# Expert stages of an eight-layer hybrid stack: 128-row tiles held in the array, weights streamed past them from a copy kept in SBUF

## The chip, the cores and the metric

One Trainium2 chip, of which one core runs the program. Matrices go through TensorE (PE, with PEld its weight loads), element work through VectorE (DVE), ScalarE (ACT) and GpSimd (POOL); SyncE (SP) starts the direct transfers. The metric is device microseconds of the whole program, the median of several runs; smaller is better.

## The reference

2048 tokens of 128 numbers pass eight layers, called a to h here: a state-space layer, experts (b), local attention with a feed-forward part, experts (d), sliding attention, full attention with experts (f), a hologram layer, full attention with experts (h). Layers b and d call the first function below with 9 experts and an inner width of 352; layers f and h end with the lines of the second one, with 8 experts, an inner width of 256, and one shared expert that every token passes.

```python
def _L0_ffn_ref(x, Wr, Wg, Wu, Wd):
    probs = jax.nn.softmax(jnp.einsum('bsh,he->bse', x, Wr), axis=-1)
    topk_w, topk_idx = jax.lax.top_k(probs, TOP_K)            # TOP_K = 2
    topk_w = topk_w / jnp.sum(topk_w, axis=-1, keepdims=True)
    cw = jnp.zeros((T, E), dtype=x.dtype).at[jnp.arange(T)[:, None], idxf].add(wf)
    gate = jax.nn.silu(jnp.einsum('th,ehi->tei', xf, Wg))
    hidden = gate * jnp.einsum('th,ehi->tei', xf, Wu)
    return jnp.einsum('tei,eih,te->th', hidden, Wd, cw).reshape(B, S, H)

# _L1_ffn_ref, after its attention
shared = swiglu(h2, sh_gate, sh_up, sh_down)
eout = jnp.einsum('etf,efd->etd', jax.nn.silu(gate) * up, e_down)
moe_out = (shared + jnp.einsum('etd,te->td', eout, combine)).reshape(B, S, d)
```

## The kernel before

Each layer is a chain of stages. A stage is one block in which every engine has its own program in a fixed, written order; engines meet through semaphores, and a stage begins when all engines have left the one before. An expert layer has these two stages:

- **norm_stage** with a router. DVE normalises 16 tiles of 128 tokens in four groups (L352 to L370), POOL takes the inverse roots (L391, L393), PE transposes the tiles (L428) and multiplies them by the router (L418), ACT copies the transposed banks (L445, L447), DVE ranks the experts (`rank`, L337 to L343). SP stores the normalised rows to `h_rows` in HBM (L1752); the stage waits for these stores. In layers f and h, ACT and POOL also split the shared expert's weights here (L452, L398), and POOL then adds the attention's result to `x` (L400).
- **experts_stage**. `dispatch` on DVE (L1919 to L1979) sorts the 4096 pairs of token and chosen expert into blocks of 256 rows of one expert, each padded at its end: 24 blocks for 9 experts, 23 for 8. It ends with two lists of row numbers per block. Then a loop over the blocks follows, in `block_steps`' order. In f and h, eight shared blocks of 256 consecutive tokens are woven in.

For one routed block b of the loop:

- POOL starts two indirect transfers that gather 128 rows each from `h_rows` (L2131), three blocks ahead (`AHEAD`), and at its end two that scatter the results to `e_rows` (L2138). POOL does `gather(b + 3)` and then `scatter(b)`.
- SP reads the block's expert into a register and loads its three matrices (L1733 to L1737) into one of three buffers (`RAW`), once block b - 3 has left the array.
- PE transposes the rows (`turn`, L1839). ACT and DVE split the turned rows into a high and a low part in the fp32r format (L1891 or L1893, L2007 or L2009), and they split the block's weights in the same way (`high_weights` L1883, `low_weights` L2000). Three passes over these parts, high by high, high by low and low by high, give a product close to fp32.
- PE computes J chunks of up to 128 inner columns (`up`, L1861): a piece of the weights is held in the array and the 256 turned rows stream past, for gate and up, three passes each, so 6 matmuls a chunk. ACT takes the silu (L1902), DVE multiplies it with up (L2018). The result lies with the inner columns on the partitions, which is what `down` (L1871) needs as its held operand.
- DVE copies the output to `rows_out` (L2032) or, for a shared block, adds it to `x` (L2028).

After the loop SP loads the scattered rows back in token order (L2062), and DVE adds them to `x` with the routing weights (L2041).

Of the kernel before, what the change touches and what calls it, by code (L numbers as in the profile page):

```python
# [60 lines left out]
BLOCK = 256  # L61
SHARED_BLOCKS = N_TOK // BLOCK
RAW = 3
GATHERS = 4
AHEAD = 3
SCATTERS = 3
# [236 lines left out]
def norm_stage(c, src, dst, rms=False, transpose=False, scale=None, shift=None, first=False, router=None, onto=None,  # L303
               shared=None):
# [20 lines left out]
    with nc.Block() as block:  # L325
# [61 lines left out]
        def _(pool):  # L387
            for g in range(CHUNKS):
# [5 lines left out]
                    .then_inc(rstd_ready.sem, 1)  # L394
            if shared is not None:
# [6 lines left out]
        if router is not None:  # L402
            @block.sync
            def _(sp):
                if shared is not None:
                    load_weights(sp, c.shared_raw, c.shared_down, shared, shared_loaded)
                store_rows(c, sp, dst)
# [14 lines left out]
        if transpose:  # L422
# [14 lines left out]
            def _(act):  # L437
                for b in range(CHUNKS):
# [10 lines left out]
                    if shared is not None and b == 0:  # L449
                        act.wait_ge(*shared_loaded.after(loads_of_expert(shared[0].shape[1]) * 16))  # L450
# [11 lines left out]
    if shared is not None:  # L462
        high_ready.passed(CHUNKS)
        shared_loaded.passed(16 * loads_of_expert(shared[0].shape[1]))
# [1244 lines left out]
def routed_blocks(E):  # L1709

    return (2 * N_TOK + E * (BLOCK - 1)) // BLOCK


def block_steps(blocks, shared):
# [3 lines left out]
    steps = [("shared", 0), ("shared", 1)]  # L1718
    done = 2
    for b in range(blocks):  # L1720
        steps.append(("routed", b))
        if b % 3 == 2 and done < SHARED_BLOCKS - 1:
            steps.append(("shared", done))
            done += 1
    return steps + [("shared", s) for s in range(done, SHARED_BLOCKS)]


def load_weights(sp, raw, down, weights, loaded):

    g, u, d = weights  # L1730
    inner = g.shape[1]
    whole = inner // P
    sp.dma_start(raw[:, 0, :], g).then_inc(loaded.sem, 16)  # L1733
    sp.dma_start(raw[:, 1, :], u).then_inc(loaded.sem, 16)
    sp.dma_start(down[:, 0:whole, :], d[0:whole * P, :].rearrange("(j p) d -> p j d", p=P)).then_inc(loaded.sem, 16)
    if inner % P:
        sp.dma_start(down[0:inner % P, whole, :], d[whole * P:inner, :]).then_inc(loaded.sem, 16)  # L1737


def loads_of_expert(inner):  # L1740

    return 3 + (1 if inner % P else 0)
# [13 lines left out]
def experts_stage(c, E, soft_of_probs, gate_w, up_w, down_w, inner, scale=None, shared=False):  # L1756
# [12 lines left out]
    COLUMNS = 2 * BLOCKS  # L1769
    LOADS = loads_of_expert(inner)  # L1770
# [4 lines left out]
    UNITS = len(steps) * J  # L1775
# [9 lines left out]
    weights_loaded = [c.count(f"moe_weights_loaded_{b}") for b in range(RAW)]  # L1785
    weights_high = c.count("moe_weights_high_ready")
# [6 lines left out]
    up_ready = c.count("moe_up_ready")  # L1793
    silu_ready = c.count("moe_silu_ready")
    hid_ready = c.count("moe_hidden_ready")
# [4 lines left out]
    links = [0]  # L1800
# [617 lines left out]
```

## Time and profile before

| | before |
|---|---|
| median of 3 runs | 2829.86 us (2827.12 to 2830.12) |
| the profiled execution | 2829.18 us, span 2827.5 us |
| PE busy | 2208.4 us (78%) |
| DVE busy | 2130.7 us (75%) |
| ACT busy | 1471.3 us (52%) |
| POOL busy | 611.3 us (22%) |
| mean granted TensorE clock | 0.865 |

The shares are means over the whole program. Nearly half of the span is the head loops of the two full attentions, in which DVE is busy all the time; the expert stages are four short stretches, and what limits them is read in those stretches alone. Spans of PE are modelled as pipelined, so a busy PE is not at its peak. A clock of 1.00 stands for 2.4 GHz, 0.50 for 1.2 GHz.

### The profile page before, as it was taken

The page shows a single profiled execution, that of the slowest core. Times are in us where ns is not written, and L with a number is a line of the kernel's source. Part 1 is how long each engine was busy: PE and PEld are TensorE (multiplying, and loading weights), DVE is VectorE, ACT ScalarE, POOL GpSimd, SP SyncE. Part 2 cuts the span into 40 slices and gives each one's busy share as a digit, 9 for nine tenths or more (in the row PEclk, how much of TensorE's full clock was granted, in tenths as well). Part 3 has the DMA queues.
Part 4 walks back from the last instruction along what each step waited for, and adds up shares of the span by engine and source line. Part 5 has one row for each costly group of instructions (what it writes and reads, how often), then busy time and mean ns, then how long its engine had stood idle before and what let it go on. Part 6 is the DMA issues. An engine that isn't in the chain of part 4 may idle for free. (4 is left out here: it accounts for less than half of the span.)

```text
span 2827.5 us, 44830 instructions
## 1 busy us (share of the span) xinstructions
PE 2208.4 (78%) x16030; PEld 983.4 (35%) x16030; DVE 2130.7 (75%) x5328; ACT 1471.3 (52%) x2014; POOL 611.3 (22%) x877
## 2 busy tenths in 40 slices
PE   6477368757558599999999976737999999999574
PEld 2376235556425312122212225622121222221474
DVE  7733687453468599999999936458999999996654
ACT  2133236323125327777777773311777777778332
POOL 5256221235411100000000014730000000000274
PEclk8578679868769769999999997865899999999698
DMA  2144272033364131101110002414010111010144
GB/s 59 46 115 123 56 128 38 13 92 116 101 102 82 19 106 24 24 13 24 24 24 12 13 18 83 120 48 123 13 24 16 21 24 24 15 22 2 44 120 118
DMA packets 133454, 154.46 MB, mean 55 GB/s; under 512 B 25674, under 2 KB 110672, under 8 KB 133232
## 3 DMA queue, kind: packets, MB, share of 16 engines
q1 hardware_dynamic: 119664, 126.30, 19.4%
q0 software_dynamic: 13568, 25.30, 3.1%
q8 instruction: 127, 2.08, 0.3%
q14 instruction: 95, 0.78, 0.1%
HBM read 106.72 MB, written 42.80 MB: 53 GB/s over the span
## 5 line engine op out<-in xcount | busy, mean ns | idle before, releaser
L1167 DVE TENSOR_REDUCE pair_mx<-ps 128x1 f32<-128x512 f32 x2048 | 1270.8, 683 | 21.6 <-PE ps L1010 17.3
L1139 ACT ACTIVATE prob<-ps 128x1024 f32<-128x1024 f32 x1024 | 990.0, 1021 | 249.7 <-PE ps L1045 248.0
L1010 PE MATMUL ps<-k_stack,q_stack 48*128 48x512 bf16 x2048 | 643.0, 404 | 56.1 <-PEq L828 13.7
L1059 PE MATMUL ps<-prob,v_head 128*32 128x512 f32 x4096 | 547.5, 607 | 1.3 <-ACT prob L1139 1.0
L1010 PEld LDWEIGHTS ps<-k_stack,q_stack 48*128 48x128 bf16 x2048 | 148.6, 93 | 903.1 <-DVE pair_mx L1167 842.1
L1045 PE MATMUL ps<-q_stack,k_stack 51*128 51x512 bf16 x2048 | 438.4, 383 | 8.7 <-ACT prob L1139 5.3
L1861 PE MATMUL ps<-block_part,weight_part 128*128 128x256 f32 (+1 forms) x1416 | 250.5, 328 | 44.8 <-DVE weight_part L2000 42.6
L1861 PEld LDWEIGHTS ps<-block_part,weight_part 128*128 128x128 f32 (+1 forms) x1416 | 215.3, 219 | 52.7 <-DVE weight_part L2000 48.8
L2138 POOL DMA_INDIRECT e_rows<-rows_out,scatter_ids x188 | 189.1, 1006 | 167.4 <-DVE rows_out L2032 129.7
L2131 POOL DMA_INDIRECT rows_in<-h_rows,gather_ids x188 | 190.0, 1011 | 156.2 <-DVE scatter_ids L1979 100.2
L2018 DVE TENSOR_TENSOR hid<-silu,ps 128x256 f32<-128x256 f32 (+1 forms) x268 | 109.7, 417 | 149.4 <-ACT silu L1902 148.7
L1190 POOL CAST shift<-rowmax 128x16 bf16<-128x16 f32 x32 | 6.3, 197 | 991.2 <-DVE rowmax L1171 991.2
L1514 DVE CUSTOM_DVE_ANT_0 ps<-ps,mask 128x256 f32<-128x256 f32 (+2 forms) x512 | 179.8, 419 | 45.1 <-PE ps L1320 42.8
L1902 ACT ACTIVATE silu<-ps 128x256 f32<-128x256 f32 (+1 forms) x268 | 98.9, 380 | 169.4 <-PE ps L1861 166.5
L2000 DVE TENSOR_TENSOR weight_part<-weight_raw,weight_part 128x352 fp32r<-128x352 f32 (+1 forms) x188 | 88.8, 473 | 128.8 <-ACT weight_part L1883 128.8
L1883 ACT ACTIVATE weight_part<-weight_raw 128x352 fp32r<-128x352 f32 (+1 forms) x188 | 85.1, 454 | 180.0 <-DMA down_raw<-in_L_ffn_Wd_dram 150.0
L1478 ACT ACTIVATE prob<-ps 128x1024 f32<-128x1024 f32 (+1 forms) x128 | 114.4, 917 | 78.2 <-PE ps L1368 78.1
L1871 PE MATMUL ps<-down_raw,hid 128*128 128x128 f32 x944 | 152.3, 320 | 3.5 <-DVE hid L2018 2.7
L1871 PEld LDWEIGHTS ps<-down_raw,hid 128*128 128x128 f32 x944 | 143.0, 234 | 8.0 <-DVE hid L2018 7.6
L1839 PE MATMUL ps<-ident,rows_in 128*128 128x128 f32 x188 | 45.7, 331 | 114.9 <-DMA rows_in<-h_rows,gather_ids 114.7
L1045 PEld LDWEIGHTS ps<-q_stack,k_stack 51*128 51x128 bf16 x2048 | 105.2, 94 | 62.7 <-ACT prob L1139 45.9
L1059 PEld LDWEIGHTS ps<-prob,v_head 128*32 128x32 f32 x4096 | 80.7, 108 | 120.5 <-issue 117.3
(233 smaller groups left out, 2038.2 us busy)
## 6 DMA issues: line engine op xcount, KB each, us to landing
k_stack<-image_dram SPq DMA_DIRECT2D x96, 192.0 KB, 4.2
q_stack<-image_dram SPq DMA_DIRECT2D x88, 192.0 KB, 4.5
weight_raw<-in_L_ffn_Wg_dram SPq DMA_DIRECT2D x48, 176.0 KB
weight_raw<-in_L_ffn_Wu_dram SPq DMA_DIRECT2D x48, 176.0 KB
results<-e_rows SPq DMA_DIRECT2D x32, 256.0 KB, 4.7
down_raw<-in_L_ffn_Wd_dram SPq DMA_DIRECT2D x48, 128.0 KB
weight_raw<-in_L_ffn_e_gate_dram SPq DMA_DIRECT2D x46, 128.0 KB
weight_raw<-in_L_ffn_e_up_dram SPq DMA_DIRECT2D x46, 128.0 KB
```

Source lines behind the costliest of these rows:

```text
L1010: nc.tensor.matmul(max_bank(n), rows_of(c.q_stack, b, g, ROWS, slice(t * P, (t + 1) * P)), rows_of(c.k_stack, b, g, ROWS, slice(k * CHUNK, ...
L1045: ins = nc.tensor.matmul(bank(c, 2 * (u % 2) + g), rows_of(c.k_stack, b, g, EXP_ROWS, slice(kb * P, (kb + 1) * P)), rows_of(c.q_stack, b, ...
L1059: ins = nc.tensor.matmul(out, c.v_head[:, e % 2, kb, :], unit, start=(kb == 0), stop=(kb == TILES - 1), skip_group_check=True)
L1139: nc.scalar.activation(c.prob[:, u % P_UNITS, :], c.ps[:, 2 * (u % 2) * CHUNK:2 * (u % 2) * CHUNK + UNIT], ACT.Exp, scale=scale).then_inc( ...
L1167: nc.vector.reduce_max(mx[:, w:w + 1], max_bank(n), AX.X).then_inc(max_taken.sem, 1)
L1478: nc.scalar.activation(probs, scores, ACT.Exp, scale=scale).then_inc(exp_done.sem, 1)
L1514: ins = nc.vector.tensor_tensor_reduce(scores, scores, c.mask32[:, window, P - back:WIDE], 1.0, LOWEST, ALU.add, ALU.max, accum_out=mx[:, ...
L1861: ins = nc.tensor.matmul(out[0:m, k * BLOCK:(k + 1) * BLOCK], w, x, start=(a == 0), stop=(a == 2))
L1871: ins = nc.tensor.matmul(bank(c, 4 + n % 2)[:, t * P:(t + 1) * P], c.hid[0:sizes[j], n % 2, j, t * P:(t + 1) * P], down_weights(n, j), sta ...
L2018: nc.vector.tensor_tensor(c.hid[0:m, n % 2, j, :], c.silu[0:m, unit % 2, :], bank(c, unit % 4)[0:m, BLOCK:2 * BLOCK], ALU.mult).then_inc(h ...
L2131: pool.indirect_dma_start(c.rows_in[:, b % GATHERS, t, :], None, c.h_rows[:, :], bass.IndirectOffsetOnAxis(ap=c.gather_ids[:, 2 * b + t:2 ...
L2138: pool.indirect_dma_start(c.e_rows[:, :], bass.IndirectOffsetOnAxis(ap=c.scatter_ids[:, 2 * b + t:2 * b + t + 1], axis=0), c.rows_out[:, b ...
```

## The change

Only the norm stages with a router and the expert stages change. A routed unit is now a tile of 128 rows of one expert: 40 tiles for 9 experts, 39 for 8, and 16 shared tiles instead of 8 shared blocks. The turned rows are held in the array and the weights stream past, so one matmul is 352 (or 256) columns long and `hid` comes out with the tokens on the partitions; it has to be transposed on PE, and copied by ACT, before `down` can use it. All experts' weights are loaded by SP in the norm stage, ahead of the stores of the rows; ACT rounds them to the high part there, and POOL subtracts to get the low part, for five experts in the norm stage and for the others at the start of the expert stage. In the loop no weights are loaded or split: PE reads the expert of each tile into a register and forms the address of the weights from it.

```diff
-BLOCK = 256
-SHARED_BLOCKS = N_TOK // BLOCK
-RAW = 3
-GATHERS = 4
-AHEAD = 3
-SCATTERS = 3
+GROUP = 3
+EARLY = 5
+GATHERS = 8
+AHEAD = 6
+SCATTERS = 5
...
+            if weights is not None:
+                for e in range(EARLY):
+                    low_weights(c, pool, e)
...
+                load_all_weights(c, sp, weights)
                 store_rows(c, sp, dst)
...
+                    if weights is not None and b:
+                        high_weights(c, act, b - 1, weights[0].shape[0], weights[0].shape[2])
...
+def high_weights(c, act, group, E, inner):
+
+    first, n = expert_groups(E)[group]
+    act.wait_ge(*c.count(f"moe_weights_loaded_{group}").after(n * loads_of_expert(inner) * 16 + 32))
+    for e in range(first, first + n):
+        c.nc.scalar.activation(c.weight_high[:, e], c.weight_raw[:, e], ACT.Copy).then_inc(c.count("moe_weights_high_ready").sem, 1)
...
+def low_weights(c, pool, e):
+
+    pool.wait_ge(*c.count("moe_weights_high_ready").after(e + 1))
+    pool.tensor_tensor(c.weight_raw[:, e].bitcast(fp32r), c.weight_raw[:, e], c.weight_high[:, e], ALU.subtract)\
+        .then_inc(c.count("moe_weights_split").sem, 1)
...
+        if n >= 0:
+            for j in range(J):
+                ins = nc.tensor.transpose(out[:, j * P:(j + 1) * P], c.hid[:, n % 2, j * P:(j + 1) * P], c.ident[:])
+        if b is not None:
+            ins = nc.tensor.transpose(out[:, 3 * P:4 * P], c.rows_in[:, b % GATHERS, :], c.ident[:])
...
+                    part = c.weight_high if v == 0 else c.weight_low
+                    x = c.block_part[:, b % 2, u, :]
+                    w = part[:, bass.ds(expert[b], 1), k, :].rearrange("p o i -> p (o i)")
+                ins = nc.tensor.matmul(bank(c, 2 * (n % 2) + k, inner), x, w, start=(a == 0), stop=(a == 2))
...
+            for n in range(N + 2):
+                if n < N:
+                    up(pe, n)
+                if n >= 2:
+                    down(pe, n - 2)
+                if any(turns(n - 1)):
+                    turn(pe, n - 1)
...
+                pool.indirect_dma_start(c.rows_in[:, b % GATHERS, :], None, c.h_rows[:, :],
+                                        bass.IndirectOffsetOnAxis(ap=c.gather_ids[:, b:b + 1], axis=0))\
+                    .then_inc(gathered[b % GATHERS].sem, 16)
...
+            for e in range(EARLY, E):
+                low_weights(c, pool, e)
             pool.wait_ge(*ids_ready.after(2))
```

Three places show how the order of instructions moves. On PE, one block of layer b in the steady part of the loop stood before as follows; the brackets name the semaphores that an instruction waits for.

```order
L1861 MATMUL ps<-block_part,weight_part 128x256 [waits moe_hidden_ready,moe_ht_split,moe_weights_split]
L1861 MATMUL ps<-block_part,weight_part 128x256 x5
L1839 MATMUL ps<-ident,rows_in 128x128 [waits moe_gathered_1]
L1839 MATMUL ps<-ident,rows_in 128x128
L1861 MATMUL ps<-block_part,weight_part 128x256 [waits moe_hidden_ready]
L1861 MATMUL ps<-block_part,weight_part 128x256 x5
L1871 MATMUL ps<-down_raw,hid 128x128 [waits moe_out_taken,moe_hidden_ready]
L1871 MATMUL ps<-down_raw,hid 128x128 x5
L1861 MATMUL ps<-block_part,weight_part 96x256 [waits moe_hidden_ready]
L1861 MATMUL ps<-block_part,weight_part 96x256 x5
```

With the change one tile, half of such a block, stands there like this (the register rows are ISA and REGISTER_ALU).

```order
L1901 ISA [waits moe_hidden_ready,moe_ht_split]
L1901 MATMUL ps<-weight_high,block_part 128x352
L1901 REGISTER_ALU
L1901 MATMUL ps<-weight_raw,block_part 128x352
L1901 MATMUL ps<-weight_high,block_part 128x352
L1916 ISA [waits moe_hidden_turned]
L1916 MATMUL ps<-down,hidt 128x128
L1916 ISA
L1916 MATMUL ps<-down,hidt 128x128
L1879 MATMUL ps<-ident,hid 128x128 [waits moe_gathered_5,moe_hidden_ready]
L1879 MATMUL ps<-ident,hid 128x128 x2
L1881 MATMUL ps<-ident,rows_in 128x128
```

(The five rows of L1901 come twice, for gate and up, and a third pair of L1916 follows the two shown.) The wait for the split weights is gone from the loop, three transposes of `hid` and seven register rows have come in, and the transposes of step n - 1 now wait for the rows of tile n + 2.

On POOL, the end of the norm stage and the start of the expert stage of layer b stood before as follows.

```order
L393 TENSOR_TENSOR rstd<-rstd,minus_half 128x4 [waits norm_rstd_ready]
L325 UNCONDITIONAL_BRANCH
L2125 UNCONDITIONAL_BRANCH [waits barrier_Pool_Activation_PE_DVE_SP_gather]
L2131 DMA rows_in<-h_rows,gather_ids 128x128 [waits moe_ids_ready]
L2131 DMA rows_in<-h_rows,gather_ids 128x128 x7
L2138 DMA e_rows<-rows_out,scatter_ids 10240x128 [waits moe_out_taken]
L2138 DMA e_rows<-rows_out,scatter_ids 10240x128
L2131 DMA rows_in<-h_rows,gather_ids 128x128 [waits moe_turned]
L2131 DMA rows_in<-h_rows,gather_ids 128x128
```

The same place with the change:

```order
L392 TENSOR_TENSOR rstd<-rstd,minus_half 128x4 [waits norm_rstd_ready]
L1770 TENSOR_TENSOR weight_raw<-weight_raw,weight_high 128x704 [waits moe_weights_high_ready] x5
L324 UNCONDITIONAL_BRANCH
L2149 UNCONDITIONAL_BRANCH [waits barrier_Pool_Activation_PE_DVE_SP_gather]
L1770 TENSOR_TENSOR weight_raw<-weight_raw,weight_high 128x704 [waits moe_weights_high_ready] x4
L2154 DMA rows_in<-h_rows,gather_ids 128x128 [waits moe_ids_ready]
L2154 DMA rows_in<-h_rows,gather_ids 128x128 x6
L2160 DMA e_rows<-rows_out,scatter_ids 9216x128 [waits moe_out_taken]
L2154 DMA rows_in<-h_rows,gather_ids 128x128
L2160 DMA e_rows<-rows_out,scatter_ids 9216x128 [waits moe_out_taken]
```

Nine subtractions have come in, five before the stage's end and four ahead of the first gather; in the loop one gather and one scatter alternate for 40 tiles, where there were two and two for 24 blocks.

On SP, the norm stage of layer b held only the stores of the rows between its two branches.

```order
L403 UNCONDITIONAL_BRANCH [waits barrier_Pool_Activation_PE_DVE_SP_release]
L1752 DMA h_rows<-h 128x4x128 [waits norm_tile_ready] x4
L325 UNCONDITIONAL_BRANCH [waits norm_rows_stored]
```

With the change the loads of the last of three groups of experts and the stores read:

```order
L1738 DMA weight_raw<-in_L_ffn_Wg_dram 128x3x352
L1739 DMA weight_raw<-in_L_ffn_Wu_dram 128x3x352
L1741 DMA down<-in_L_ffn_Wd_dram 128x2x128
L1743 DMA down<-in_L_ffn_Wd_dram 96x128
L1741 DMA down<-in_L_ffn_Wd_dram 128x2x128
L1743 DMA down<-in_L_ffn_Wd_dram 96x128
L1741 DMA down<-in_L_ffn_Wd_dram 128x2x128
L1743 DMA down<-in_L_ffn_Wd_dram 96x128
L1786 DMA h_rows<-h 128x4x128 [waits norm_tile_ready] x4
```

So 24 loads stand ahead of the four stores, on the same queue, and the stage still waits for the stores.

## Rows read from the trace of the kernel before

**Rows 1.** The head of the page: the span of the profiled execution.
```profile
span 2827.5 us, 44830 instructions
```

**Rows 2.** Loops b, d, f, h: PE, PEld, DVE, ACT, POOL busy, clock, DMA, GB/s.
```profile
127.78:295.98 168.20, 118.42 (x768) 112.22 (x768) 67.08 (x171) 51.79 (x143) 98.59 (x96) 0.79 0.36 105
588.50:760.56 172.06, 118.80 (x768) 112.98 (x768) 66.56 (x171) 51.79 (x143) 96.42 (x96) 0.79 0.36 103
1721.85:1854.57 132.72, 99.14 (x659) 91.50 (x657) 62.57 (x170) 49.28 (x133) 91.89 (x92) 0.86 0.36 105
2677.25:2804.03 126.78, 92.92 (x651) 85.92 (x649) 61.78 (x169) 49.30 (x133) 90.21 (x90) 0.92 0.37 109
```

**Rows 3.** Groups by line and form: busy, mean ns | idle before, released by.
```profile
L2138 POOL DMA_INDIRECT e_rows<-rows_out,scatter_ids x188 | 189.1, 1006 | 167.4 <-DVE rows_out L2032 129.7
L1883 ACT ACTIVATE weight_part<-weight_raw 128x352 fp32r<-128x352 f32 x96 | 47.3, 494 | 153.3 <-DMA down_raw<-in_L_ffn_Wd_dram 150.0 <-PE ps L1861 3.3
L2018 DVE TENSOR_TENSOR hid<-silu,ps 128x256 f32<-128x256 f32 x220 | 91.7, 417 | 86.4 <-ACT silu L1902 85.7
```

**Rows 4.** Timeline of POOL in layer b: start, us, [idle before].
```profile
127.78 1.22 POOL L2131 DMA_INDIRECT rows_in<-h_rows,gather_ids  x1 [25.30 <-DVE scatter_ids L1979]
143.36 1.00 POOL L2138 DMA_INDIRECT e_rows<-rows_out,scatter_ids  x1 [5.53 <-DVE rows_out L2032]
295.01 0.97 POOL L2138 DMA_INDIRECT e_rows<-rows_out,scatter_ids  x1 [0.30 <-issue]
```

**Rows 5.** Timeline of PE's weight loads in layer b, at both clocks.
```profile
143.26 1.42 PEld L1871 LDWEIGHTS ps<-down_raw,hid 128*128 128x128 f32 x12
144.61 0.75 PEld L1861 LDWEIGHTS ps<-block_part,weight_part 128*96 128x96 f32 x6
...
206.72 0.29 PEld L1839 LDWEIGHTS ps<-ident,rows_in 128*128 128x128 f32 x2 [3.53 <-DMA rows_in<-h_rows,gather_ids]
206.99 1.40 PEld L1861 LDWEIGHTS ps<-block_part,weight_part 128*128 128x128 f32 x6
208.28 1.88 PEld L1871 LDWEIGHTS ps<-down_raw,hid 128*128 128x128 f32 x10
```

**Rows 6.** Short stretches: columns as in rows 2; the last is the results' reload.
```profile
142.00:144.00 2.00, 2.00 (x19) 2.00 (x19) 0.75 (x2) 0.29 (x1) 0.64 (x1) 1.00 0.77 233
148.00:150.00 2.00, 0.28 (x3) 0.08 (x1) 0.25 (x1) 0.42 (x2) 1.39 (x3) 0.57 0.58 149
206.00:208.00 2.00, 1.27 (x6) 1.28 (x7) 0.93 (x3) 1.32 (x4) 1.52 (x2) 0.50 0.17 51
299.00:301.00 2.00, 0.00 (x0) 0.00 (x0) 0.00 (x0) 0.00 (x0) 0.00 (x0) 0.50 1.02 279
```

**Rows 7.** DVE and POOL working on SBUF at once; ns least/median/most by line.
```profile
46.53 4.78 POOL L509 TENSOR_TENSOR x<-x,row_L_attn_a_ln_beta 128x2048 f32<-128x2048 f32 x1
L633 DVE TENSOR_TENSOR big<-big x8: 683/692/4982, 45.9 to 74.9; 128x512 f32<-128x512 f32 x8
L398 POOL TENSOR_TENSOR shared_part<-shared_raw,shared_part x4: 720/730/734, 1691.2 to 2647.3; 128x256 fp32r<-128x256 f32 x4
```

**Rows 8.** Timeline: starts of the norm and the expert stage (b, then h).
```profile
93.78 0.49 DVE L352 BATCH_NORM_STATS2 bn<-x 128x6 f32<-128x128 f32 x2 [0.55 <-PEq L676]
110.16 0.19 DVE L1919 TENSOR_SCALAR iota_high<-iota 128x48 f32<-128x48 f32 x1 [0.34 <-PEq L325]
...
2637.13 0.87 DVE L352 BATCH_NORM_STATS2 bn<-h 128x6 f32<-128x128 f32 x4 [0.32 <-PEq L1615]
2660.20 0.19 DVE L1919 TENSOR_SCALAR iota_high<-iota 128x46 f32<-128x46 f32 x1
```

**Rows 9.** SP's queue in layer b; one register row lies before L1737.
```profile
116.39 0.37 SPq L1734 DMA_DIRECT2D weight_raw<-in_L_ffn_Wu_dram  x1
116.85 0.38 SPq L1735 DMA_DIRECT2D down_raw<-in_L_ffn_Wd_dram  x1
117.42 0.34 SPq L1737 DMA_DIRECT2D down_raw<-in_L_ffn_Wd_dram  x1
```

More of the change, by code:

```diff
@@ L1717, in block_steps @@
         return [("routed", b) for b in range(blocks)]
-    steps = [("shared", 0), ("shared", 1)]
-    done = 2
+    steps = [("shared", t) for t in range(3)]
     for b in range(blocks):
         steps.append(("routed", b))
[L1722 to L1725, printed above, removed]
+        if b % 3 == 2:
+            steps.append(("shared", 3 + b // 3))
+    return steps
@@ L1740, in loads_of_expert @@
 def loads_of_expert(inner):
-    return 3 + (1 if inner % P else 0)
+    return 1 + (1 if inner % P else 0)
 def store_rows(c, sp, src):
@@ L1896, in silu @@
-    def silu(act, n, j):
-        unit = n * J + j
-        m = sizes[j]
-        act.wait_ge(*up_ready.after(unit + 1))
-        if unit >= 2:
-            act.wait_ge(*hid_ready.after(unit - 1))
-        nc.scalar.activation(c.silu[0:m, unit % 2, :], bank(c, unit % 4, BLOCK)[0:m], ACT.Silu).then_inc(silu_ready.sem, 1)
+        for j in range(J):
+            m = sizes[j]
+            if kind == "shared":
+                w = c.shared_down[0:m, j, :]
+            else:
+                w = c.down[0:m, bass.ds(expert[b], 1), j, :].rearrange("p o d -> p (o d)")
+            ins = nc.tensor.matmul(bank(c, 6 + n % 2, D), c.hidt[0:m, n % 2, j, :], w, start=(j == 0), stop=(j == J - 1))
@@ new lines, in down, with turned_count, evacuate @@
+        ins.then_inc(out_ready.sem, 1)
+    def turned_count(n):
+        return n + 4 - sum(1 for k in range(-3, n + 1) if not any(turns(k)))
+    def evacuate(act, n):
+        if not any(turns(n)):
+            return
+        act.wait_ge(*turned.after(turned_count(n)))
+        out = bank(c, 4 + n % 2)
+        b = routed_at(n + 3)
+        if b is not None:
+            if scale is None:
+                ins = nc.scalar.activation(c.block_part[:, b % 2, 0, :], out[:, 3 * P:4 * P], ACT.Copy)
+            else:
+                ins = nc.scalar.activation(c.block_part[:, b % 2, 0, :], out[:, 3 * P:4 * P], ACT.Identity, scale=scale, bias=0.0)
+            ins.then_inc(ht_high.sem, 1)
+        if n >= 0:
+            if n >= 2:
+                act.wait_ge(*out_ready.after(n - 1))
+            nc.scalar.activation(c.hidt[:, n % 2, :, :].rearrange("p j t -> p (j t)"), out[:, 0:WHOLE], ACT.Copy)\
+                .then_inc(hidt_ready.sem, 1)
@@ L1904, in router_scalar, with silu @@
+    def silu(act, n):
+        act.wait_ge(*gate_ready.after(n + 1))
+        if n >= 2:
+            act.wait_ge(*hid_ready.after(n - 1))
+        nc.scalar.activation(c.silu[:, n % 2, :], bank(c, 2 * (n % 2), inner), ACT.Silu).then_inc(silu_ready.sem, 1)
     def router_scalar(act):
```

299 lines of the change are left out of this document (129 added, 170 removed).

## The prediction, on record before the changed kernel ran

> **What bounds the kernel now.** The profiled execution took 2829.18 us, of which the span is 2827.5 [rows 1] and 1.7 lie around it; it stands 0.7 below the median of the runs, so the sum is made against 2829.2. I read the busy time of the four expert loops first, because the change touches nothing else but the two stages around each. From the first gather to the last scatter they take 168.2, 172.1, 132.7 and 126.8 us, 600 in all [rows 2]. No engine fills them: PE is busy 70% of loop b, DVE 40%, ACT 31%.
>
> Then the groups by line and the chain of waits. In b and d the rounding of a block's weights on ACT waits 150 us in all for the block's transfer [rows 3]; PE then waits too, and its clock falls: the granted clock was 1.00 at 142 us, 0.57 at 148 us with PE busy 0.28 of 2 us, and 0.50 at 206 us after a wait of 3.53 us for rows [rows 5, 6]. The mean is 0.79 in b and d, 0.86 and 0.92 in f and h [rows 2]. In f and h POOL is what is left: one indirect transfer costs it 1.006 us and 0.30 of issue, 1.31 in all [rows 3, 4], and a block needs four. 92 of them are 120 us out of the 126.8 of loop h. In b 96 of them are 126 of 168.2.
>
> **The loops.** With tiles, each needs one gather and one scatter: 80 in b and d, 78 in f and h (before 96 and 92).
>
> POOL's floor: the first scatter came 15.6 us after the first gather [rows 4]. Until then the new order runs two turned tiles, three `up` and one `down`, about as many columns as before, with one gather less to wait for: 14 us. Seven gathers fit into these. The 73 transfers left in b and d take 73 x 1.31 = 95.6. At the end the last tile still has to land, be turned and pass two steps of PE, while POOL works off scatters: I take 3.4 for the part that sticks out and 1.0 for the last scatter. That is **114 us** for b and d. In f and h it is 14 + 71 x 1.31 + 4.4 = 111, and 112 with the shared steps woven in.
>
> PE's floor, at clock 1.00: six high-low matmuls went at 0.125 each with 256 columns [rows 5]; 352 columns give at most 0.172, so `up` is 1.03 us. A `down` of 128 columns costs two instructions of 1.35 / 12 = 0.113, so three cost 0.68; a transpose took 0.145 at the half clock [rows 5] and is taken as 0.11 here, four as 0.44. That makes 2.15 us a tile, below POOL's 2.62. In f and h a routed tile is 0.75 + 0.45 + 0.33 = 1.53, a shared one 1.42, together 82 us for 39 and 16. ACT has a silu, the split and the copy of the turned `hid`: 0.49 for 352 columns [rows 3] thrice at most, 1.5. DVE has 0.417 x 352 / 256 = 0.57 and two short ones, some 1.2. No wait closes a loop: gather(b + 6) starts three tiles before PE turns it, which is 7.9 us at POOL's pace, and it lands within 4.
>
> Does the clock hold? PE would be busy 2.15 of 2.62 us, with gaps under 1 us instead of 3.5. Loop h, at 0.92, is the nearest row [rows 2]. At 0.50 an `up` of 256 columns took 1.29, a `down` pair 0.38, a transpose 0.15 [rows 5]; a tile would be 1.77 + 1.13 + 0.60 = 3.5. With nine tenths at the upper level the mean is 2.3, still below 2.62. So POOL sets the pace. By the Trainium skill (TensorE: Matmul & The Clock Gate, "HAM oscillation") it is waits between bursts that send the array back to its half clock; by this rule the loops would run at 1.00, and the trace agrees as far as its falls stand behind such waits (3.53 us).
>
> Change: b -54.2, d -58.1, f -20.7, h -14.8, together **-147.8**. The bound from below is 1.25 us a transfer (0.95 with nothing in its way) instead of 1.31, another -17.
>
> **The norm stages.** SP now loads 4.87 MB (9 experts) or 3.15 MB (8) ahead of the stores of 1.05 MB. The reload of the results moved 279 GB/s with all 16 engines busy [rows 6]; at 285, 4.87 MB take 17.1 us and the stores 3.7. With 2 us to start and 1 to land the stage of b takes 24 to 25 us, where it took 16.4 [rows 8]: **+8.5** each in b and d. That cover, the stage itself, is used up: ACT's copies (nine of about 0.8, two of them ahead of a bank that PE waits for) and five subtractions end before it. In f and h the loads end at 14 us and the stores at 19, inside the 23.1 us that the stage has [rows 8]. There POOL comes late instead: five subtractions of 1.27 us stand ahead of the sum into `x`.
>
> What a subtraction costs others: one on POOL took 0.73 for 256 columns, so near 1.68 for 704 and 1.27 for 512. While POOL's 4.78 us addition ran at 46.5 us, a DVE operation on two SBUF tiles took 4.98 instead of 0.69 [rows 7]: it waited the whole POOL instruction out. The Trainium skill (GPSIMD Engine Reference, Key points) says that POOL shares its SBUF interfaces with VectorE and that DVE instructions with two SBUF inputs contend. The page gives no size; the trace has one, 4.3 us. For f and h I take **+3** each, between 0 (DVE's last normalisation is no longer caught behind the sum) and +6. The same page (Engine selection) advises against element work on POOL, about twice as slow as DVE with two inputs; by it the split of the weights would be in the wrong place.
>
> **The dispatch.** Four subtractions (6.7 us) in b and d, three (3.8) in f and h start with the stage, together with DVE's `dispatch`, which is what the first gather waits for (17.6 us, from 110.16 to 127.78 [rows 4, 8]). DVE's operations there are short and mostly read SBUF, so each can be caught behind a subtraction. Bounds are 0 and 6.7 (0 and 3.8). I take 5.5 and 3, near the upper end because the one row of such an encounter shows the whole wait, less 0.7 for smaller one-hot tables: **+4.8** twice, **+2.3** twice. PE's loading of expert numbers lies in its wait for those tables.
>
> **Sum.** -147.8 + 17 + 6 + 9.6 + 4.6 = -110.6; 2829.2 - 110.6 = **2719 us**.
>
> **The rivals.**
>
> *PE's sequencer sets the pace.* No row shows a register operation on PE. On SP one costs 0.57 - 0.47 = 0.10 between two issues [rows 9]. A tile of b has seven, a routed one of f six. Hidden behind matmuls they cost nothing; wholly exposed, a tile takes 2.15 + 0.7 = 2.9 us, over POOL's 2.62. Then loop b is 42 steps of 2.9 and 6.5 for start and end, 128 us, and loop f 39 x 2.23 + 16 x 1.5 + 6.5 = 118: 40 us more in all, **2759**. For it speaks that the row stands right at the wait; against it, that the next matmul is 0.17 long.
>
> *The stages around cost nothing.* If DVE gets through between subtractions and the loads flow at 340 GB/s, the +37 outside the loops shrink to about +7: **2689**.
>
> *PE stays at the half clock.* The one that ends slower. If the short wait for rows in every tile keeps the granted clock at 0.50 through the loops, a tile of b costs 3.5 and loop b 42 x 3.5 + 6.5 = 154, loop f 39 x 2.5 + 16 x 2.35 + 6.5 = 142. That is 40 more in b and d each and 30 in f and h: 2719 + 140 = **2859**. It decides once four fifths of the tiles run so. For it speak 0.79 in b and d; against it, that there the waits were 3.5 us, and that PE, once it is the bound, waits for nobody.
>
> **How the numbers follow.** Forecast (POOL paces, stages pay) 0.68, with 2695 to 2750 as its own range; sequencer 0.15; stages free 0.12; half clock 0.05. The range runs from 2680, under the third case and part of POOL's lower bound, to 2785, which takes the second case in with some of the clock's. Faster by over 0.2% (5.7 us, about what a measurement can tell from no change) 0.94, within 0.2% 0.01, slower 0.05.
>
> **What would show it.** In the new trace the loops should last 110 to 118 us, gather and scatter follow each other at 1.3 us with "issue" before them, PE's turn of rows wait for the gather at about 0.4 us a tile, and the clock stand over 0.9. The norm stages of b and d should last about 25 us with the stores last; DVE's first operations of the dispatch should show 1.7 us where they had 0.2 to 0.3. I am wrong if scatters wait for `rows_out` all through the loop (PE or ACT sets the pace), or if the register rows leave gaps ahead of L1901 and L1916.

## The result, and the profile after

The changed kernel took 2682.5 us (2681.0 to 2687.3) against 2830.0 of the kernel before beside it: ratio 0.9481, 95% interval 0.9465 to 0.9498. That is 36.5 us under the forecast of 2719 and 2.5 us inside the lower end of the range. The profiled execution took 2681.46 us. The head of its profile page, to be read against [rows 1]:

```profile
span 2679.7 us, 44826 instructions
PE 2154.3 (80%) x15840; PEld 914.9 (34%) x15840; DVE 2093.9 (78%) x5208; ACT 1471.6 (55%) x2036; POOL 592.2 (22%) x851
```

The loops b, d, f, h from the first gather to the end of the last scatter, with the columns of [rows 2]:

```profile
138.94:246.27 107.33, 94.50 (x640) 84.29 (x640) 44.10 (x122) 42.55 (x121) 78.20 (x80) 0.97 0.17 50
548.42:655.95 107.53, 94.31 (x640) 84.28 (x640) 44.03 (x122) 42.55 (x121) 78.18 (x80) 0.97 0.16 49
1622.64:1726.84 104.20, 94.45 (x692) 84.38 (x691) 50.79 (x157) 49.23 (x151) 76.28 (x78) 0.98 0.17 50
2555.04:2658.99 103.95, 94.55 (x692) 84.42 (x691) 50.78 (x157) 49.32 (x151) 76.22 (x78) 0.98 0.17 50
```

The loops fell by 60.9, 64.5, 28.5 and 25.6 us, 179.5 together. (The last window of [rows 2] ends before the last two scatters; loop h lasted 129.6 us in the kernel before, not 126.8.) The granted clock rose from 0.79, 0.79, 0.86 and 0.92 to 0.97 and 0.98. POOL's timeline in loop b (start, us, idle before and its releaser) shows what paces it, and where the end of the loop is spent:

```profile
149.57 1.00 POOL L2160 DMA_INDIRECT e_rows<-rows_out,scatter_ids  x1 [1.91 <-DVE rows_out L2076]
...
177.79 0.99 POOL L2160 DMA_INDIRECT e_rows<-rows_out,scatter_ids  x1 [0.30 <-issue]
179.08 0.97 POOL L2154 DMA_INDIRECT rows_in<-h_rows,gather_ids  x1 [0.30 <-issue]
180.36 0.99 POOL L2160 DMA_INDIRECT e_rows<-rows_out,scatter_ids  x1 [0.30 <-issue]
...
236.79 0.97 POOL L2160 DMA_INDIRECT e_rows<-rows_out,scatter_ids  x1 [0.30 <-issue]
239.49 0.96 POOL L2160 DMA_INDIRECT e_rows<-rows_out,scatter_ids  x1 [1.73 <-DVE rows_out L2076]
245.31 0.96 POOL L2160 DMA_INDIRECT e_rows<-rows_out,scatter_ids  x1 [0.96 <-DVE rows_out L2076]
```

From 149.57 to 236.79 a transfer starts every 1.28 us with nothing but "issue" ahead of it: POOL has no slack, 2.56 us a tile. Only the last four scatters wait for results.

Around the loops the program became longer. DVE and POOL at the start of the expert stage of b, against [rows 8]:

```profile
115.96 6.70 POOL L1770 TENSOR_TENSOR weight_raw<-weight_raw,weight_high 128x704 fp32r<-128x704 f32 x4 [4.01 <-POOLq L324]
116.08 1.58 DVE L1966 TENSOR_SCALAR iota_high<-iota 128x40 f32<-128x40 f32 x1
117.58 0.17 DVE L1967 CAST top_f<-top_i 128x32 f32<-128x32 uint32 x1
117.79 3.35 DVE L1969 TENSOR_TENSOR pick<-iota,top_f 128x144 f32<-128x144 f32 x2
121.16 1.66 DVE L1971 TENSOR_TENSOR both<-pick 128x144 bf16<-128x144 f32 x1
122.74 0.23 DVE L1972 TENSOR_SCALAR spare<-iota_high,part 128x40 f32<-128x40 f32 x1
```

Four DVE operations each end with one of POOL's four subtractions of 1.68 us: L1966 took 1.58 us where its forerunner had taken 0.19 [rows 8], and only the CAST slipped through between two of them. From the start of the expert stage to the first gather it is now 22.86, 22.84, 19.84 and 19.86 us (17.62, 17.62, 17.05 and 17.05 before), +16.1 together. The norm stages, from the first DVE operation to the first of the expert stage, take 22.0, 21.1, 26.2 and 26.2 us (16.4, 16.4, 23.1 and 23.1 before), +16.6. The balance of the spans is -179.5 + 16.1 + 16.6 = -146.8, and the spans differ by 147.8; 1 us lies in other stages.

### The profile page after: what moved, and what is told of

The parts are those of the page before. It is cut to its first block and busy times, and to the rows that moved or that the text cites. A ratio compares the mean times of both kernels' runs of the same rounds, so it can differ in the third digit from the quotient of the medians.

```text
span 2679.7 us, 44826 instructions
## 1 busy us (share of the span) xinstructions
PE 2154.3 (80%) x15840; PEld 914.9 (34%) x15840; DVE 2093.9 (78%) x5208; ACT 1471.6 (55%) x2036; POOL 592.2 (22%) x851
## 3 DMA queue, kind: packets, MB, share of 16 engines
q1 hardware_dynamic: 82000, 98.27, 16.8%
q8 instruction: 131, 2.15, 0.3%
## 5 line engine op out<-in xcount | busy, mean ns | idle before, releaser
L1017 PEld LDWEIGHTS ps<-k_stack,q_stack 48*128 48x128 bf16 x2048 | 148.6, 93 | 901.9 <-DVE pair_mx L1174 842.2
L2154 POOL DMA_INDIRECT rows_in<-h_rows,gather_ids x158 | 153.2, 970 | 111.7 <-DVE scatter_ids L2026 64.8
L1901 PE MATMUL ps<-weight_high,block_part 128*128 x632 | 174.2, 328 | 0.0
L2160 POOL DMA_INDIRECT e_rows<-rows_out,scatter_ids x158 | 155.7, 985 | 67.2 <-issue 36.9
L1916 PE MATMUL ps<-down,hidt 128*128 (+1 forms) x792 | 129.5, 294 | 8.9 <-ACT hidt L1940 3.8
L1327 PE MATMUL ps<-k_stack,q_stack 48*128 48x256 bf16 (+2 forms) x512 | 52.1, 286 | 82.3 <-DVE pair_mx L1521 41.4
L1901 PEld LDWEIGHTS ps<-weight_high,block_part 128*128 128x128 f32 x632 | 114.4, 193 | 0.2
L1916 PEld LDWEIGHTS ps<-down,hidt 128*128 128x128 f32 (+1 forms) x792 | 100.5, 190 | 32.5 <-issue 28.9
L2063 DVE TENSOR_TENSOR hid<-silu,ps 128x256 f32<-128x256 f32 (+1 forms) x190 | 87.0, 459 | 29.5 <-ACT silu L1947 28.9
L1879 PE MATMUL ps<-ident,hid 128*128 128x128 f32 x460 | 83.6, 278 | 24.4 <-DMA rows_in<-h_rows,gather_ids 16.9
L433 PE MATMUL ps<-ident,n 128*128 128x128 f32 x96 | 27.6, 445 | 89.9 <-DVE n L367 49.3
```

The source lines that it names most:

```text
L1017: nc.tensor.matmul(max_bank(n), rows_of(c.q_stack, b, g, ROWS, slice(t * P, (t + 1) * P)), rows_of(c.k_stack, b, g, ROWS, slice(k * CHUNK, ...
L1901: ins = nc.tensor.matmul(bank(c, 2 * (n % 2) + k, inner), x, w, start=(a == 0), stop=(a == 2))
L1916: ins = nc.tensor.matmul(bank(c, 6 + n % 2, D), c.hidt[0:m, n % 2, j, :], w, start=(j == 0), stop=(j == J - 1))
L2063: nc.vector.tensor_tensor(c.hid[:, n % 2, 0:inner], c.silu[:, n % 2, :], bank(c, 2 * (n % 2) + 1, inner), ALU.mult).then_inc(hid_ready.sem, 1)
L2154: pool.indirect_dma_start(c.rows_in[:, b % GATHERS, :], None, c.h_rows[:, :], bass.IndirectOffsetOnAxis(ap=c.gather_ids[:, b:b + 1], axis=0))\
L2160: pool.indirect_dma_start(c.e_rows[:, :], bass.IndirectOffsetOnAxis(ap=c.scatter_ids[:, b:b + 1], axis=0), c.rows_out[:, b % SCATTERS, :], ...
```

## The experiments

All lengths are from the first gather to the last scatter, for loops b, d, f, h. Medians and ratios are against the kernel before, run beside each.

| run | loops, us | total, us | ratio (95%) |
|---|---|---|---|
| before | 168.2, 172.1, 132.7, 129.6 | 2830.0 | 1 |
| changed | 107.3, 107.5, 104.2, 104.0 | 2682.5 | 0.948 (0.947 to 0.950) |
| e1_fixed_expert | 106.3, 107.2, 103.6, 103.8 | 2680.6 | 0.948 (0.946 to 0.951) |
| e2_no_scatter | - | 2654.9 | 0.939 (0.936 to 0.941) |
| e3_no_scatter_fixed | - | 2641.4 | 0.934 (0.931 to 0.936) |
| e4_no_reload | 164.5, 164.5, 132.2, 132.2 | 2822.3 | 0.997 (0.995 to 0.999) |
| e5_before_ahead | 134.4, 137.9, 119.6, 119.3 | 2738.3 | 0.968 (0.966 to 0.971) |
| e6_before_ahead_no_reload | 128.2, 128.8, 120.6, 120.0 | 2725.1 | 0.964 (0.962 to 0.967) |
| e7_after_ahead3 | 325.4, 327.4, 150.0, 152.2 | 3216.3 | 1.137 (1.134 to 1.140) |
| e8_dve_late | 108.4, 108.9, 106.6, 106.6 | 2672.2 | 0.945 (0.943 to 0.948) |
| e9_splits_moved | 109.6, 110.6, 104.9, 104.8 | 2659.8 | 0.941 (0.940 to 0.943) |
| e10_ahead4 | 148.6, 147.2, 112.3, 112.6 | 2784.6 | 0.986 (0.983 to 0.988) |
| e11_ahead5 | 128.8, 128.3, 140.0, 141.6 | 2798.5 | 0.966 (0.964 to 0.969) |
| e12_ahead5_again | 110.4, 114.6, 106.7, 107.8 | 2699.0 | 0.954 (0.951 to 0.957) |

**What PE has in hand: e1, e2, e3.** In e1 and e3 PE's expert numbers are constants, and the pass over the low half of the weights reads the high half again:

```diff
-                _, values = nc.values_load_multi_w_load_instructions(c.block_expert[0:1, ...], ...)
-                expert.extend(values)
+            expert.extend(b * E // BLOCKS for b in range(BLOCKS))
...
-                    w = part[:, bass.ds(expert[b], 1), k, :].rearrange("p o i -> p (o i)")
+                    w = c.weight_high[:, expert[b], k, :]
```

> The changed kernel, but PE takes the expert of each tile from a list fixed in the program (b * E // BLOCKS) and not from registers; the pass with the low half of the weights reads the high half instead, so the choice of expert and the low part of the weights are left out, with the same number and size of matmuls. Theory (POOL's transfers pace the loops at 1.28 us each, 2.56 a tile, and PE has 0.36 us a tile to spare): the loops stay at 107 and 104 us, the total within 2 us of the changed kernel's 2682. Rival (the register rows are what PE and with it the loop waits for): 0.1 to 0.3 us less in each tile, 4 to 12 us less in each loop, 2645 to 2665 in all.

In e2 (and e3) SP stores the results and POOL only gathers:

```diff
+            for b in range(BLOCKS):
+                sp.wait_ge(*out_taken.after(step_of[b] + 1))
+                sp.dma_start(c.e_rows[b * P:(b + 1) * P, :], c.rows_out[:, b % SCATTERS, :])
...
-                scatter(b)
```

> The changed kernel, but the tiles' results are stored by SP with direct transfers in the order of the tiles, 40 or 39 of them; the placing of the results by row number is left out. POOL keeps the gathers alone, 1.28 us a tile. Theory (POOL paces, PE is next): PE's own period shows, 2.20 us a tile in b and d and 6.97 for three routed and one shared in f and h; loops of b and d 98 to 101 us instead of 107.4, of f and h 100 to 102 instead of 104, the total 18 to 24 us less, 2658 to 2664. Rival (PE's chain with its transposes and copies already sets the pace, the even spacing of POOL only follows it): loops change by under 2 us, total 2676 to 2682. Second rival (a gather's landing sets it): the same.

> Both edits together: no indirect scatters, and the expert from a fixed list. Here nothing of POOL hides PE. Theory (register rows are mostly hidden behind matmuls of 0.16 us; the starts of a tile's six up matmuls lie 0.25, 0.16 and 0.20 us apart where 352 columns alone take 0.16): 0.05 to 0.15 us less a tile than without scatters alone, 2 to 6 us less in b and d, 0 to 3 in f and h, 4 to 16 less in all. Rival (the register rows stand fully exposed, as my second case of the prediction had it): 0.4 us and more a tile, over 16 us less in each loop, over 50 in all.

e1 changed nothing that can be measured. e2 gained 27.6 us over the changed kernel, somewhat more than expected, and POOL now waits for PE. From the first gather to SP's last store the loops take 96.9, 97.0, 99.1 and 99.2 us, and in e3 92.8, 92.9, 95.9 and 96.0. POOL's timeline in loop b of e2:

```profile
181.94 0.94 POOL L2158 DMA_INDIRECT rows_in<-h_rows,gather_ids  x1 [1.26 <-PE ps L1881]
184.15 0.94 POOL L2158 DMA_INDIRECT rows_in<-h_rows,gather_ids  x1 [1.26 <-PE ps L1881]
186.35 0.94 POOL L2158 DMA_INDIRECT rows_in<-h_rows,gather_ids  x1 [1.26 <-PE ps L1881]
```

The period is PE's, 2.20 us, against 2.56 with scatters. With fixed experts as well (e3) the turns on PE follow at 2.12 us, and 13.5 us more are gone: the register rows cost 0.08 us a tile, and only once POOL is out of the way. So POOL paces the changed kernel, with PE 0.36 us a tile behind it.

**What the kernel before waited for: e4, e5, e6.** e4 leaves the stream of weights out of the kernel before:

```diff
-            for b in range(BLOCKS):
+            for b in range(RAW):
                 e = sp.value_load(c.block_expert[0:1, b:b + 1], min_val=0, max_val=E - 1)
...
-            act.wait_ge(*weights_loaded[b % RAW].after((b // RAW + 1) * LOADS * 16))
+            act.wait_ge(*weights_loaded[b % RAW].after(LOADS * 16))
```

> The kernel before, but SP loads the weights of the first three blocks of each expert layer only, and later blocks use what lies in the three buffers: the stream of weights is left out, all splits, transfers of rows and matmuls stay. Theory (in b and d the weight stream was the bound and POOL's 96 transfers of 1.31 us come next; in f and h POOL's 92 were nearly the bound): loops of b and d 168 and 172 down to 132 to 140, f 133 to 124 to 128, h 129.6 to 124 to 129; the total 65 to 85 us less than before, 2745 to 2765. Rival (the stream was hidden, and what the change brought came from smaller padding and from the swap of operands): under 10 us less, 2820 and up.

This fell short by far: 3.6 us instead of 65 to 85. ACT's wait for the transfers was gone, and PE now waited for rows instead: 41.3 us in loop b, where it had waited 24.4 for rows and 21.3 for split weights. PE and POOL in loop b of e4:

```profile
184.16 0.96 PE L1861 MATMUL ps<-block_part,weight_part 128*128 128x256 f32 x6
184.95 1.50 PE L1871 MATMUL ps<-down_raw,hid 128*128 128x128 f32 x12
186.21 1.66 PE L1861 MATMUL ps<-block_part,weight_part 128*96 128x256 f32 x12
191.46 0.69 PE L1839 MATMUL ps<-ident,rows_in 128*128 128x128 f32 x2 [3.59 <-DMA rows_in<-h_rows,gather_ids]
191.79 1.63 PE L1861 MATMUL ps<-block_part,weight_part 128*128 128x256 f32 x6
```

```profile
184.94 1.02 POOL L2138 DMA_INDIRECT e_rows<-rows_out,scatter_ids  x1 [3.67 <-DVE rows_out L2032]
186.28 0.98 POOL L2138 DMA_INDIRECT e_rows<-rows_out,scatter_ids  x1 [0.30 <-issue]
187.56 0.99 POOL L2131 DMA_INDIRECT rows_in<-h_rows,gather_ids  x1 [0.31 <-issue]
188.86 0.96 POOL L2131 DMA_INDIRECT rows_in<-h_rows,gather_ids  x1 [0.30 <-issue]
```

Read together, they are a ring, a chain of waits that comes back to its start. POOL waits 3.67 us for a block's result; behind its two scatters stand the two gathers of a later block; they land at 191.4; PE has waited 3.59 us for them, its clock has fallen (six matmuls take 1.63 us, and took 0.96 at 184.16), and the next result is late. A block takes 6.85 us and POOL is at work for 5.2 of them: it has time left, but cannot start a gather while the scatter ahead of it in its queue waits. That formed a new theory, with AHEAD as the number to change in the kernel before:

```diff
-GATHERS = 4
-AHEAD = 3
+GATHERS = 8
+AHEAD = 6
```

> The kernel before with its gathers six blocks ahead in eight buffers instead of three in four; weights reloaded as before. Without the reload PE still waited 3.6 us for rows in every second block of loop b and the loop kept its length, so a ring is suspected: gather(b + 4) stands behind scatter(b) on POOL, two scatters and two gathers are 5.2 us and the landing 2.5, 7.7 in all, against some 1.2 blocks of 6.9 us that PE needs to get to the turn. Theory of two rings (rows, and weights: load of block b behind the down of b - 3): this edit opens the first only, ACT's wait for weights is left, b and d fall little, by 0 to 12 us each, f and h by 0 to 8; total 2790 to 2825. Rival (the ring of rows is the only bound): b and d down to 135 to 145, f and h to 124 to 128, total 2745 to 2765. Rival (no ring at all, the rows are late for want of bandwidth): no change.

> The kernel before with gathers six blocks ahead in eight buffers, and weights loaded for the first three blocks of each expert layer only, so the choice of expert is left out for the others. Theory of two rings: both are open, and POOL's transfers remain: 96 of 1.29 us and some 12 for start and end, loops of b and d 134 to 140, f and h 122 to 128, total 2745 to 2765, clock in the loops over 0.9. Rival (the blocks of 256 rows with weights held in the array are limited on PE or in the chain of silu and hid): loops of b and d stay over 155, total over 2790.

These two constants alone bring the kernel before from 2827 to 2738 us. The row ring was the bound, and the guess in the expectation of e5 that weights formed a second one of equal length was wrong: with the rows early, the reload costs only 6.2 and 9.1 us in b and d, and -0.9 and -0.7 in f and h. With both gone (e6) loop b is 128.2 us for 96 transfers, 1.33 each: POOL's floor, as in the changed kernel. (Most follow at 1.29; in many blocks one takes 1.63, where a scatter of 1.32 us fell beside DVE's subtraction of weights.)

**The same number in the changed kernel: e7, e10, e11, e12.** AHEAD is 3, 4 and 5 instead of 6 and nothing else is touched. It counts tiles here and blocks of two tiles in the kernel before: 6 tiles are as many rows ahead as its 3 blocks were, and 3 tiles are half of them.

> The changed kernel with AHEAD 3 instead of 6, nothing else. Theory of the ring of rows: from scatter(b) over gather(b + 4), landing 2.4 us, turn, four steps of PE to its output and back to scatter(b + 4) it is some 1.3 + 1.3 + 2.4 + 1.2 + 4 x 2.2 + 0.5 = 15.5 us for four tiles, 3.9 us a tile instead of 2.56: b and d 40 to 60 us longer each, f and h 20 to 50, total 2800 to 2900, so all of the gain can go with the lookahead alone. Rival (lookahead does not matter, POOL paces anyway): total within 5 us of 2682.

> The changed kernel with AHEAD 4, nothing else. With 3 each tile of loop b took 8.4 us: the turn in the step after down(b) wants the rows of b + 4, whose gather stands behind scatter(b), and from the end of down(b) to that turn 4.6 us passed (0.6 to the scatter, 1.3 for it, 2.7 for the gather and its landing). Theory of the ring: with 4 this chain has one step of PE beside it, so a tile takes 4.6 us instead of 2.56; loops of b and d 180 to 195 us, of f and h 110 to 130, total 2835 to 2910. With 5 the chain would be shared by two steps, 2.3 a tile, below POOL's 2.56, so 6 has one step in hand. Rival (the cost of a short lookahead is that of the clock at its half level, which comes or goes as a whole): either near 2682 or near 3216, nothing between.

> The changed kernel with AHEAD 5, nothing else. With 3 a tile of loop b took 8.4 us, with 4 it took 3.45 (6.9 for two, of which PE waited 2.0 once), with 6 it takes 2.56. Theory of the ring: a chain of about 4.6 us from the end of down(b) to the turn that wants the rows behind scatter(b) has one more step of 2.2 us beside it each time; with 5 it is shared by two steps and falls below POOL's 2.56, so the loops stay at 107 and 104 to within 3 us and the total at 2680 to 2690. Rival (lookahead pays on without a threshold, each step of it half of the last): loops of b and d 120 to 130, total 2700 to 2740.

> The same kernel with AHEAD 5 once more, since beside the last run the kernel before itself took 2900 us instead of 2825 and ACT stood still for 2.5 to 3 us in every fourth tile, released by nothing of this core. If the ring with its threshold holds: loops of b and d 106 to 110 us, of f and h 103 to 107, total 2680 to 2692. If lookahead pays on without a threshold: b and d 120 to 130, total 2700 to 2740.

With 3 the changed kernel is slower than the one before by 13.7%, much worse than I had worked out. PE and POOL in loop b of e7:

```profile
206.23 1.16 PE L1916 MATMUL ps<-down,hidt 128*128 x6
211.95 0.87 PE L1879 MATMUL ps<-ident,hid 128*128 128x128 f32 x3 [4.57 <-DMA rows_in<-h_rows,gather_ids]
```

```profile
207.99 0.99 POOL L2160 DMA_INDIRECT e_rows<-rows_out,scatter_ids  x1 [6.12 <-DVE rows_out L2076]
209.28 0.97 POOL L2154 DMA_INDIRECT rows_in<-h_rows,gather_ids  x1 [0.31 <-issue]
```

I had spread the chain over four tiles. But `turn` stands right behind `down(b)` in PE's order and wants the rows of tile b + 4, whose gather stands right behind scatter(b) in POOL's. So output, scatter, gather and landing, 4.6 us, lie bare in every tile. As PE idles there, the mean clock of loop b is 0.62 and PE's own part takes 3.8 us instead of 2.2: 8.4 us a tile. This is the half-clock rival of the prediction, made real by the lookahead. By the Trainium skill (TensorE: Matmul & The Clock Gate, "HAM oscillation") waits between bursts bring the array back to its half clock; this trace agrees (0.59 from 165 to 225 us, with 4.6 us of wait in every tile).

With 4 a tile takes 3.45 us (6.9 for two, with 2.0 us of wait in every second), less than the 4.6 expected, at a mean clock of 0.93 over the loop and 0.97 from 165 to 225 us. With 5, e11 says little: beside it the kernel before took 2900 us, and ACT stood still for 2.5 to 3 us at a time with no cause inside the core. Repeated as e12, the loops are 3.1, 7.1, 2.5 and 3.9 us longer than with 6, 16.5 us in all (7.4 of them are a longer wait of POOL for the first result), while POOL runs at 1.28 us a transfer nearly throughout. The total of 2699.0 misses the 2680 to 2692 expected and lies at the lower end of the rival's 2700 to 2740; the loops are far below the rival's 120 to 130. So the threshold is there, but soft: at 5 the ring costs little in the steady part and still costs at the start and now and then. At 6 no transfer in the middle of the loop waits. More than 6 was not run.

**The cost around the loops: e8, e9.** e8 moves the subtractions of the expert stage from POOL to DVE, behind the dispatch:

```diff
             dispatch(dve, chain)
+            for e in range(EARLY, E):
+                low_weights(c, dve, e)
             router_vector(dve, chain)
...
-            for e in range(EARLY, E):
-                low_weights(c, pool, e)
```

> The changed kernel, but the four or three subtractions that POOL does at the start of the expert stage are done by DVE after the dispatch, where it has 3.4 us without work until the first rows are turned. Theory (POOL's subtractions hold DVE up): the dispatch goes back to 17.6 and 17.0 us, 5.2 less in b and d and 2.8 less in f and h; DVE needs about 0.8 us for each of 704 columns, 3.1 for four, hidden in the 3.4; total 14 to 17 us less than the changed kernel, 2665 to 2668. Rival (the dispatch grew because its tables for 40 tiles are larger): dispatch 22 us still, total 2682 to 2685.

The dispatch fell to 17.25 and 16.77 us, so POOL's hold on DVE was its whole growth. Four subtractions took DVE 3.29 us (0.82 each, where POOL takes 1.68). The total fell by 10 us, not 14 to 17: the loops grew by 1.1, 1.3, 2.4 and 2.6 us. In f and h the first shared tile's `hid` now stands behind DVE's longer list; and the first gather of a loop, beside DVE's subtractions, took POOL 1.58 us in b and 1.31 in h, where it had taken 1.21 and 1.14. The norm stages of f and h stayed at 26.2.

e9 also moves everything out of the norm stage:

```diff
-                load_all_weights(c, sp, weights)
-                store_rows(c, sp, dst)
+                load_all_weights(c, sp, weights, 0, 2)
+                store_rows(c, sp, dst, lambda: load_all_weights(c, sp, weights, 2, 3))
...
-                    if weights is not None and b:
-                        high_weights(c, act, b - 1, weights[0].shape[0], weights[0].shape[2])
...
         def _(act):
+            for g in range(len(expert_groups(E))):
+                high_weights(c, act, g, E, inner)
             router_scalar(act)
...
+        low_weights(c, dve, 0)
         dve.wait_ge(*prefix_ready.after(1))
```

> The changed kernel with the work around the loops laid out again. SP loads the weights of six experts first, then stores the rows as they come, then loads the rest; ACT rounds all weights at the start of the expert stage, not between its copies of the norm stage; all subtractions are DVE's, one in each of its two waits of the dispatch, the others after the dispatch (in layers f and h behind the first two shared tiles' hid). Theory (the norm stages grew because ACT's copies and the stores stood behind the loads, and because POOL's subtractions held DVE up, the dispatch by the latter alone): norm stages of b and d 16.4 to 17.5 us instead of 21 to 22, of f and h 23.1 instead of 24.6; dispatch 17.3 to 17.8 and 16.8 to 17.1; loops of b and d 2 to 3.5 us longer, as seven subtractions of 0.8 us meet 3.4 us without work; the total 18 to 30 us less than the changed kernel, 2652 to 2664. Rival (the loading itself takes the time: 4.87 MB at some 325 GB/s are 15 us wherever they stand, and the expert stage waits for them instead): norm stages shorter but dispatch or first tile later by the same, total 2666 to 2680, no better than with four subtractions moved to DVE (2672).

The norm stages came down to 17.7, 16.7, 23.1 and 23.1 us, the dispatch to 17.3 and 16.8, and the loading hid behind the dispatch; the rival falls. (The 24.6 us that the expectation gives for f and h in the changed kernel leaves out their first 1.6 us.) At 2659.8 us, 0.9410 of before (0.9396 to 0.9425), it is the fastest complete kernel of the study. One trace line each from the changed kernel and from e9 shows the stores of the rows:

```profile
108.34 3.55 SPq L1786 DMA_DIRECT2D h_rows<-h  x4
```

```profile
102.61 2.69 SPq L1781 DMA_DIRECT2D h_rows<-h  x4
```

In the changed kernel 24 loads were issued ahead of them, from 94.03 to 108.34, 0.60 us each. But the last four tiles were ready no sooner than 108.0, as POOL's subtractions held up DVE there as well (5.21 us for the four, 1.12 in e9, as before):

```profile
102.80 5.21 DVE L369 TENSOR_SCALAR h<-x,mv,rstd 128x128 f32<-128x128 f32 x4 [0.47 <-POOL rstd L392]
```

A third cause is the transfers themselves. From 96 to 112 us the DMA engines of the changed kernel had no pause (share 1.09, at 329 GB/s):

```profile
96.00:112.00 16.00, 11.12 (x48) 9.60 (x48) 14.51 (x76) 6.46 (x10) 12.79 (x12) 0.50 1.09 329
```

ACT waited for the last weights until 112.67, and the stage, which waits for the stores behind them, ended at 115.9. All three causes are near one length, and e9 takes them away together; how much each alone would cost cannot be told from it.

## Why the prediction was right, and where its steps were off

**Direction and mechanism of the new loops: right.** POOL sets the pace, at 1.28 us a transfer where I had 1.31; PE's floor for a tile of b was given as 2.15 us and is 2.20 (e2); the clock is 0.97. Of the sign that PE would wait 0.4 us a tile for rows less than half showed: 4.0 us from 165 to 225 us, in some 23 tiles. The size was less sure than the mechanism: 2682.5 lies under the 2695 to 2750 that I had given to this very case, and inside the whole range only because its lower end had been set for the rival of free stages. That part is luck.

**The size of the loops: 31.7 us too long in all.** 2.8 of that is the truncated window of loop h. For b, 14 + 73 x 1.31 + 4.4 = 114 was measured as 10.6 + 73 x 1.28 + 3.4 = 107.4: the first scatter comes 10.6 us after the first gather (3.4 less), the slot is 0.03 shorter (2.2 less), the end 1.0 shorter. The mis-sized term is the fill: I had taken the 15.6 us of the old order [rows 4] and shortened them by one gather only. No run isolates which part of it the smaller tiles made shorter.

**What bounded the kernel before: wrong in its cause.** I put the length of loops b and d on ACT's wait for the weights and the fallen clock, and called POOL "what is left" in f and h. The wait was real in the rows and not the bound: without the reload the program was 3.6 us shorter (e4). What closed the loop was the ring over scatter, gather and turn with AHEAD 3; 115 us of PE's waits for rows were in the trace of the kernel before, in a row that the prediction did not use:

```profile
L1839 PE MATMUL ps<-ident,rows_in 128*128 128x128 f32 x188 | 45.7, 331 | 114.9 <-DMA rows_in<-h_rows,gather_ids 114.7
```

The forecast came out near all the same, because it was built from the new floor and not from what the removal of each wait would give. In terms of the runs, the loops' 179.5 us are: 91 for opening the ring (e5), 14 for the resident weights once that is open (e6 against e5), and 75 from e6 to the changed kernel, where 60 transfers fewer by 1.29 us make 77. The split holds for this order of the edits: taken first, the missing reload is worth 9 us in the loops and 4 in the total (e4). And e5 opens the ring with twice the rows ahead, while the changed kernel has as many as the kernel before and opens it with one gather and one scatter in turn; that this is worth the same 91 us there is not shown.

**"No wait closes a loop": right, and the line that everything hung on.** It was a remark of one sentence on AHEAD 6, with 7.9 us against 4. With 3 that wait closes, and the changed kernel is 389 us slower than the one before (e7).

**The norm stages: +23 predicted, +16.6 measured.** For b and d I had 17.1 us for the bytes and 3.7 for the stores, +8.5 each; they are +5.6 and +4.8. The mis-sized term is the rate: 329 GB/s from 96 to 112 us, where I had 285. With it the prediction's own sum gives 18.0 + 3 = 21.0 us (an estimate) of the 22.0 that b took. Beside the bytes stand the issue of 24 loads, 14.3 us, and DVE's held-up last group. In f and h the stages are 3.1 us longer, where I had +3, and by the mechanism that I had given: POOL's sum into `x` starts 17.4 us into the stage of h instead of 10.8, and a DVE operation that meets it takes 3.79 us instead of 0.68.

```profile
2526.39 4.94 POOL L402 TENSOR_TENSOR x<-x,h 128x2048 f32<-128x2048 f32 x1
2528.08 3.79 DVE L336 TENSOR_TENSOR ht_part<-ht,ht_part 128x512 fp32r<-128x512 f32 x1
```

**The dispatch: +14.2 predicted, +16.1 measured,** with the mechanism of [rows 7]; e8 shows it by taking it away. By the Trainium skill (GPSIMD Engine Reference, Key points) DVE instructions with two SBUF inputs contend with POOL. The trace agrees for L1969 and L1971. L1966 has one tile as its input and was held too; the page's other case, a 2-port mode, may be that, but the trace names no modes.

**The rivals.** The sequencer rival fell: its 0.7 us a tile are 0.08. The rival of free stages named 2689 us, nearest of all to the result, but not for its reason: the stages cost 32.7 us, and the loops gave more. The half clock came only with a short lookahead; and by the prediction's own 3.5 and 2.15 us a tile it would set the pace once a third of the tiles ran so, not four fifths.

## What to carry to other kernels

When an in-order queue holds both the gather of a later tile and the scatter of this one, follow the ring from a result over that queue back to the next load before crediting a wait to bandwidth; a lookahead constant may be worth more than the rest of a rewrite (89 us of 2827 here, where the changed kernel is another 56 below that), and a rewrite into smaller tiles needs a larger one, counted in tiles. To find what bounds a loop, leave the suspected stream out: a wait that takes its place, of the same length, shows the real bound. Put element work on POOL only where DVE has nothing to do, and transfers that nobody waits for behind those that end a stage.

## What the runs showed of the hardware

- An indirect transfer of 128 rows of 512 bytes costs POOL 0.96 to 0.99 us and 0.30 of issue in the steady part of the changed kernel's loops, an even 1.28 us from start to start. Beside a DVE subtraction of two SBUF tiles it took longer: 1.32 us in e6, 1.58 in e8.
- A DVE operation that meets a POOL operation of two SBUF tiles ends with it: 1.58 us for 128x40 numbers, where 128x48 took 0.19, 1.68 instead of 0.27 for 128x144; a CAST of 128x32 numbers went through in 0.17. Four subtractions of 128x704 numbers moved off POOL (e8) gave 5.6 us back.
- The same subtraction of 128x704 numbers takes 1.68 us on POOL and 0.82 on DVE.
- PE's addressing through registers cost 0.08 us in a tile of layer b or d, all of it hidden while POOL paced.
- The granted clock followed the waits. From 165 to 225 us, in loop b, it was 0.59 with 4.6 us of wait in every tile of 8.4 us, 0.97 with 2.0 us in every second tile, and 1.00 with waits of up to 1.3 us now and then. The means of the whole loops (0.62, 0.93, 0.97) also hold their first 6 us or so at 0.50.
